# Attention and ternary feed-forward on one core: weights ahead of x rows, a second Y bank in slot 0, 32-column first-token products, M's source stored in halves, no layer norm tensor

## The reference, cut to what matters

```python
qkv = x @ w_qkv                      # 16 heads of 64; token 0 is a "first token" seen by all
# blocks of 16 tokens attend to the first token and to a causal window of their own and two
# earlier blocks (the mask leaves no later key)
attn = softmax(q k / 8)              # over the window
attn = einsum('gh,bhnij->bgnij', w_th, attn)
out  = (attn @ v) @ w_out + b_out    # row 0 of the result: v[:, 0] @ w_out + b_out
x1 = layernorm(x + out)              # eps 1e-5
h  = gelu(ternary_linear(x1, w_up))  # divides x1 by its rms + 1e-8, weights are -1, 0 or 1
y  = layernorm(x1 + ternary_linear(h, w_down))
```

## Time and profile before

| | us |
|---|---|
| median of 3 runs | 256.18 (255.93 to 256.25) |
| the profiled execution, its own time | 257.67 |
| its span, first to last instruction | 255.8 |
| PE busy in the span | 231.0 (90%) |
| DVE busy | 182.9 (72%) |
| ACT busy | 162.7 (64%) |
| POOL busy | 91.7 (36%) |
| mean granted TensorE clock | 0.978 |

### The profile page before, as it was taken

How to read it: one execution, slowest core, us unless ns; L and a number is a source line. 1 busy time by engine, 2 the same in 40 slices (tenths; PEclk the granted TensorE clock), 3 DMA queues, 4 the chain that set the end, 5 groups by cost and what they waited for, 6 DMA issues and landing times.

```text
span 255.8 us, 9953 instructions
## 1 busy us (share of the span) xinstructions
PE 231.0 (90%) x4307; PEld 206.9 (81%) x4307; DVE 182.9 (72%) x485; ACT 162.7 (64%) x311; POOL 91.7 (36%) x110
## 2 busy tenths in 40 slices
PE   7798999999999999999999899988999977899930
PEld 6697988988999898889888798877887756799920
DVE  0743689987776984688567856789568888886960
ACT  2584366687566459766887479754974444875940
POOL 7035123522322251626452543424252633012350
PEclk9999799999999999999999999999999999999995
DMA  7627560020020002010101020001001001000011
GB/s 225 194 77 222 181 162 5 3 63 3 3 55 12 23 4 67 0 24 12 54 4 41 8 65 0 23 25 40 27 0 46 3 3 42 3 12 13 3 44 41
DMA packets 18911, 11.69 MB, mean 46 GB/s; under 512 B 2036, under 2 KB 17972, under 8 KB 18740
## 3 DMA queue, kind: packets, MB, share of 16 engines
q1 hardware_dynamic: 18016, 9.94, 13.6%
q10 hardware_dynamic: 852, 1.12, 1.3%
HBM read 8.91 MB, written 2.10 MB: 43 GB/s over the span
## 4 chain that ended last, share of the span: by engine, by line
PE 50%; DVE 21%; ACT 18%; issue 4%; DMA 2%; POOL 1%; SPq 0%; POOLq 0%; DVEq 0%; ACTq 0%
PE bank L1078 8%; PE bank L1080 7%; PE bank L1079 7%; DVE CTl L851 6%; PE bank L1227 5%; PE bank L1201 5%; ACT CTh L557 3%; DVE AT L856 3%; DVE E L865 3%; ACT L648 3%; PE bank L1185 2%; DMA w_sb<-in_L_attn_w_qkv 2%; ACT Yb L557 2%; ACT E L700 2%; DVE mx L863 2%
## 5 line engine op out<-in xcount | busy, mean ns | idle before, releaser
L851 DVE TENSOR_TENSOR CTl<-bank,CTh 128x512 fp32r<-128x512 f32 x64 | 41.1, 684 | 24.2 <-ACT CTh L557 24.0
L500 POOL TENSOR_TENSOR E<-E,rc 128x400 f32<-128x400 f32 x32 | 27.9, 872 | 82.8 <-DVE rc L873 82.8
L557 ACT ACTIVATE Yb<-bank 128x512 f32<-128x512 f32 x64 | 38.5, 601 | 29.6 <-PE bank L1080 29.2
L1078 PE MATMUL bank<-xTh,Gh 128*128 128x256 f32 x128 | 40.2, 314 | 3.4 <-ACT Yb L557 2.2
L700 ACT ACTIVATE E<-E 128x400 f32<-128x400 f32 x32 | 17.3, 540 | 38.5 <-DVE E L865 38.4
L1078 PE MATMUL bank<-CTh,Mh 128*128 128x256 f32 x128 | 36.7, 287 | 1.8 <-DVE CTl L851 1.8
L1080 PE MATMUL bank<-xTh,Gl 128*128 128x256 f32 x128 | 36.2, 283 | 0.0
L1079 PE MATMUL bank<-xTl,Gh 128*128 128x256 f32 x128 | 36.1, 282 | 0.0
L557 ACT ACTIVATE CTh<-bank 128x512 fp32r<-128x512 f32 x64 | 34.7, 599 | 1.9 <-PE bank L1227 1.8
L1079 PE MATMUL bank<-CTl,Mh 128*128 128x256 f32 x128 | 35.7, 279 | 0.0
L1080 PE MATMUL bank<-CTh,Ml 128*128 128x256 f32 x128 | 35.7, 279 | 0.0
(11 more groups left out here) (142 smaller groups left out, 478.3 us busy)
## 6 DMA issues: line engine op xcount, KB each, us to landing
raw<-in_L_attn_x SPq DMA_DIRECT2D x37, 64.0 KB
pt_rows<-PT SPq DMA_DIRECT2D x1, 1024.0 KB, 6.2
R<-pt_rows SPq DMA_DIRECT2D x1, 1024.0 KB, 6.3
xr<-in_L_attn_x SPq DMA_DIRECT2D x6, 128.0 KB
out<-y SPq DMA_DIRECT2D x6, 128.0 KB, 1.8
raw<-in_L_attn_x SPq DMA_DIRECT2D x12, 56.0 KB
w_sb<-in_L_attn_w_qkv ACTq DMA_DIRECT2D x2, 256.0 KB, 4.7
w_sb<-in_L_attn_w_qkv SPq DMA_DIRECT2D x2, 256.0 KB, 5.1
```

What stands on the lines that cost most here:

```text
L500: tt(e, e, rc[s % 2][:, :].unsqueeze(2).broadcast_to([P, TILES, WIN]), ALU.mult).then_inc(s_norm, 1)
L557: copy = lambda o, i, **k: nc.scalar.activation(o, i, ACT.Copy, **k)
L851: v.tensor_tensor(ct_view(CTl[s // 4 % 2], s % 4, q), c_view(s, q), ct_view(f32(CTh[s // 4 % 2][:, :, :]), s % 4, q), ALU.subtract).then_i ...
L1078: mm(o, wh, rh, start=start, stop=False, **k)
```

## The change

Five parts. (1) On SP, w_up and w_down are loaded before the waits and transfers of `window(0, 0)`. (2) In slot 0 the second query part goes to bank 3 (`y_bank`), and the waits of `queries(0, 0)` and `queries(0, 1)` ask for one Yb copy less. (3) "v0" and "bos" use pieces of 32 columns. (4) PT is stored by two transfers of 8 heads each, the first of which waits for the first two pieces only. (5) The layer norm tensor is not formed. x1n is kept (two buffers, and two more for chunks 6 and 7), y2 = x1n * weight + down, with weight = (hroot + 1e-8) * ratio: y2 is the old one times hroot + 1e-8, and the second norm adds `floor` = 1e-5 * hden squared to the variance in place of 1e-5. `residual` makes both root inputs in one instruction and both roots are now square roots; `input_scale` has two instructions for four; `layernorm` and its calls are gone.

```diff
-            sp.wait_ge(s_eva, read_no("A", "p", 2))
-            sp.wait_ge(s_evd, read_no("D", "p", 3))
-            sp.dma_start(pt_rows.rearrange("g o c -> o g c"), PT[:, :, :]).then_inc(s_pt, 16)
-            sp.wait_ge(s_pt, 16)
+            for half in range(2):
+                sp.wait_ge(s_eva, read_no("A", "p", 2 * half))
+                sp.wait_ge(s_evd, read_no("D", "p", 2 * half + 1))
+                hs = slice(8 * half, 8 * half + 8)
+                sp.dma_start(pt_rows[hs].rearrange("g o c -> o g c"), PT[:, hs, :]).then_inc(s_pt, 16)
+            sp.wait_ge(s_pt, 32)
...
+        def y_bank(s, b):
+            return Y_BANK[b if s == 0 else 0]
...
-                    pe.wait_ge(s_Ye, 8 + 2 * s + b)
+                    pe.wait_ge(s_Ye, 8 + 2 * s + b - (s == 0))
                     c = (s // 4 + 1) % 6
-                    y_part(Y_BANK[0], slice(c * CHUNK, c * CHUNK + CHUNK), 4 * (s % 4) + 2 * b)
+                    y_part(y_bank(s, b), slice(c * CHUNK, c * CHUNK + CHUNK), 4 * (s % 4) + 2 * b)
...
-                            for lo in (0, 64):
+                            for lo in range(0, P, 32):
                                 c = P * k + lo
-                                ins = mm(bnk[lo:lo + 64, 2 * k:2 * k + 2], w_sb[2][:, c:c + 64], x0T[:, :],
+                                ins = mm(bnk[lo:lo + 32, 2 * k:2 * k + 2], w_sb[2][:, c:c + 32], x0T[:, :],
...
-                v.tensor_scalar(var_in[n % 2][:, 0, :], mv[n % 2][:, :, 1], EPS_LN, None, ALU.add).then_inc(f_vin, 1)
-                v.tensor_copy(var_in[n % 2][:, 1, :], mv[n % 2][:, :, 1]).then_inc(f_vin, 1)
+                v.tensor_tensor(var_in[n % 2][:, :, :], mv[n % 2][:, :, 1].unsqueeze(1).broadcast_to([P, 2, CT]), eps_ln[:, :, :],
+                                ALU.add).then_inc(f_vin, 1)
...
-                for i in range(CT):
-                    v.scalar_tensor_tensor(out=rms[:, i:i + 1], in0=roots[n % 2][:, 1, i:i + 1], scalar=roots[n % 2][:, 0, i:i + 1],
-                                           in1=eps_rms[:, i:i + 1], op0=ALU.mult, op1=ALU.add).then_inc(f_rms, 1)
-                dve.wait_ge(f_rms, CT * (n + 1))
-                v.reciprocal(inv[:, :], rms[:, :]).then_inc(f_inv, 1)
-                dve.wait_ge(f_inv, n + 1)
-                v.tensor_tensor(rn[:, :], inv[:, :], roots[n % 2][:, 0, :], ALU.mult).then_inc(f_rn, 1)
+                v.scalar_tensor_tensor(out=roots[n % 2][:, 1, :], in0=roots[n % 2][:, 0, :], scalar=EPS_RMS,
+                                       in1=roots[n % 2][:, 1, :], op0=ALU.mult, op1=ALU.add).then_inc(f_den, 1)
+                dve.wait_ge(f_den, n + 1)
+                v.reciprocal(scales[n % 2][:, :, :], roots[n % 2][:, :, :]).then_inc(f_scales, 1)
...
+                v.tensor_tensor(ratio[:, n % 4, :], roots[n % 2][:, 1, :], scales[n % 2][:, 0, :], ALU.mult).then_inc(f_ratio, 1)
...
+                dve.wait_ge(f_ratio, n + 1)
+                v.scalar_tensor_tensor(out=weight[:, :], in0=hroot[:, :], scalar=EPS_RMS, in1=ratio[:, n % 4, :],
+                                       op0=ALU.add, op1=ALU.mult).then_inc(f_weight, 1)
                 v.tensor_scalar(hden[:, :], hroot[:, :], EPS_RMS, None, ALU.add).then_inc(f_hden, 1)
-                dve.wait_ge(f_hden, n + 1)
-                v.reciprocal(hinv[:, :], hden[:, :]).then_inc(f_hinv, 1)
-                dve.wait_ge(f_hinv, n + 1)
-                dve.wait_ge(f_x1, CT * (n + 1))
+                dve.wait_ge(f_weight, n + 1)
...
-                    v.scalar_tensor_tensor(out=y2[own(n)][:, i:i + 1, :], in0=dn_bank(n)[:, P * i:P * i + P].unsqueeze(1),
-                                           scalar=hinv[:, i:i + 1], in1=res[own(n)][:, i:i + 1, :],
+                    v.scalar_tensor_tensor(out=y2[own(n)][:, i:i + 1, :], in0=x1n[own(n)][:, i:i + 1, :],
+                                           scalar=weight[:, i:i + 1], in1=dn_bank(n)[:, P * i:P * i + P].unsqueeze(1),
                                            op0=ALU.mult, op1=ALU.add).then_inc(f_y2, 1)
+                dve.wait_ge(f_hden, n + 1)
+                v.scalar_tensor_tensor(out=floor[:, :], in0=hden[:, :], scalar=EPS_LN, in1=hden[:, :],
+                                       op0=ALU.mult, op1=ALU.mult).then_inc(f_floor, 1)
```

More of the change, by code:

```diff
@@ L105, in attention_ffn @@
         attnS = sb("attnS", [P, CHUNK])
-        res = [sb(f"res{i}", [P, CT, P]) for i in range(2)]
-        x1n = sb("x1n", [P, CT, P])
+        res = sb("res", [P, CT, P])
+        x1n = [sb(f"x1n{i}", [P, CT, P]) for i in range(2)]
         x1Th = sb("x1Th", [P, CHUNK], F32R)
@@ L118, in attention_ffn @@
         roots = [sb(f"roots{i}", [P, 2, CT]) for i in range(2)]
-        rms, inv, rn, hss, hroot, hden, hinv, var2 = [sb(name, [P, CT]) for name in (
-            "rms", "inv", "rn", "hss", "hroot", "hden", "hinv", "var2")]
+        scales = [sb(f"scales{i}", [P, 2, CT]) for i in range(2)]
+        ratio = sb("ratio", [P, 4, CT])
+        hss, hroot, hden, weight, floor, var2 = [sb(name, [P, CT]) for name in (
+            "hss", "hroot", "hden", "weight", "floor", "var2")]
         rstd2 = [sb(f"rstd2_{i}", [P, CT]) for i in range(2)]
```

69 lines of the change are left out of this document (32 added, 37 removed).

## The result

| | before | after |
|---|---|---|
| median, 20 runs each, us | 256.34 (255.71 to 259.68) | **253.97** (252.66 to 257.69) |
| profiled execution, us | 257.67 | 253.67 |
| its span | 255.8 | 251.9 |
| mean granted clock | 0.978 | 0.979 |

The ratio is 0.9894, 95% interval 0.9869 to 0.9918: 2.4 us faster, where 2.6 was the forecast.

The account below looks back on a forecast made before the run. PE was taken to bound most slots, DVE the feed-forward steps and slots 29 and 30. Front 1.4, DVE 1.0 and end 0.2 make 2.6 us off the median 256.18: 253.6, range 252.0 to 255.3 (8 in 10).

Parts of the forecast that it names:

- the front: Start to slot 4: PE 2.65 us earlier, rows 0.7 later, slack 2.08, so a 1.27 stall and net gain 1.4.
- Second Y bank, 32 columns: PE in slots 0 and 1: the bank gains 0.85 and costs 0.35; shorter v0 and bos gain 0.65.
- The clock, 1.5: PE from 26.5 to 29.5 us: the clock stays at 2.4 GHz instead of half that, gain 1.5 us.
- The order on SP, and what waits for it: SP's loads: PT lands 0.7 us later, delaying R and chunk 1's raw rows; PE stalls 1.27 in slot 4.
- 32 columns: gain 0.65: PE's v0 and bos: 64 small pieces take 0.70 us instead of 1.02 each, gain 0.65 together.
- DVE's steps, 1.0: Feed-forward steps in slots 12, 20, 24, 28 and 30: shorter DVE work gains 1.0 us, bounds 0.5 and 1.6.
- The end, 0.2: The last two `second_sum` on DVE, behind PE's down_back: a shorter chain gains 0.2 us.
- The rows are not late: Rival, 21%: PT lands some 0.6 us sooner, PE's 2.65 arrives in full; 252.3.
- The clock falls again: Rival, 6%: low clock behind the 1.27 stall in slot 4 costs 1.5 us more; 255.1.
- DVE's savings are absorbed: Rival, 12%: shorter DVE steps only lengthen its wait for ACT's copies; 254.6.
- small pieces cost as now: Rival, 3%: v0's and bos's 64 pieces stay at 32 ns, 2.04 us each; 255.0.
- SP stands behind the 127-row piece: Rival, 8%: that issue takes 5.65 us; PT, R and raw rows come 4.6 late; 1.3 slower, 257.5.

Follow-up runs that it names:

- e04: The kernel before with only SP's order changed, w_up and w_down loaded ahead of the raw rows: 256.56 us, ratio 0.9989.
- e02: The kernel before with parts 1 to 4 (SP order, second bank, 32 columns, PT in halves), layer norm as before: 257.25 us, ratio 0.9990.
- e12: The changed kernel with products nobody reads put where PE idled in slots 29 and 30: 253.94 us, ratio 0.9892.
- e17: e07 with the two layer norm instructions put back in each of five chunks, as instructions nobody waits for: 254.77 us, ratio 0.9866.
- e14: e10 with the first token's products back on 64 columns: 252.28 us, ratio 0.9796.
- e07: The changed kernel with the first token's products (v0, bos) back on 64 columns: 252.80 us, ratio 0.9862.
- e10: The changed kernel with DVE's `ratio` and, for chunks 0 to 3, `floor` moved into its wait for the exponential: 251.91 us, ratio 0.9841.
- e03: The kernel before with the second bank in slot 0 and the 32 columns alone: 256.27 us, ratio 0.9971.
- e11: The changed kernel with slot 4's raw rows issued while SP waits for PT to land: 253.72 us, ratio 0.9903.
- e01: The kernel before with part 5 alone (DVE's, no layer norm tensor): 254.65 us, ratio 0.9915.

## Why the prediction was right, point by point

The total was right, 253.97 for 253.6, inside the range, and in good part by luck: the front alone gave nothing for 1.4, DVE's part 2.1 for 1.2, and the two errors cancel.

- **Second Y bank, 32 columns.** Right as mechanisms: no idle ahead of `queries(0, 1)`, v0 at 0.71 for 0.70, and 2.93 less from slot 0 to slot 4, for a PE that was to be 2.65 earlier. (In absolute time PE took up slot 4's transposes 1.76 earlier, at 39.70 for 41.46: 0.61 had gone ahead of slot 0 and 0.30 into the idle of slot 3.) The row of small pieces decided against the Trainium skill's overhead of each matmul (TensorEngine Tiling (Array Packing), "Performance Considerations"), by which v0 would have taken longer, not shorter; the trace gives 11 ns a piece.
- **The clock, 1.5.** It was at 1.00 in slots 0 and 1, as said, but the reason given does not hold: e04 kept the idle of 0.69 and the 1.10 of v0, and stayed at 1.00 as well. Either the low clock belongs to an execution, or the order alone removes it; one profile of each cannot tell. If the first, the sum counts it twice, once within the front's gain and its slack of 2.08, and once in the 1.49 taken off for the median. An estimate for an execution of before without it: PE takes up slot 4's transposes 1.5 earlier, the slack is 0.58, and 0.58 - 0.7 is -0.1 for the front, where e02's median gain cannot be told from zero.
- **The order on SP, and what waits for it.** Partly right. R was issued at 27.69 in e12, 28.15 in after, 29.52 in e17 and 31.26 in e02; the forecast was one number, 29.7, for what varies by over 3 us. By the prediction's own list, R before 29 was a sign of being wrong, and after's 28.15 is one. The stall stood in slot 4 in e02 (1.39), e17 (1.75), e14 (0.59) and e07 (0.31), and not in after, e10 and e12. So "net gain of the front 1.4" is the step that failed: what an execution keeps in slots 0 to 4 went from 2.93 (after) over 2.15 (e03), 0.92 (e04) and -0.57 (e02) to -0.97 (e11), and in medians the front alone gives 256.75 - 257.25, nothing, with an interval of -0.5 to +1.1 us.
- **What the step left out** is that 64 more records put other work at the boundaries of PE's instruction packets. No rival named it. In slots 2 and 3 of the kernels with 32 columns PE idled 0.30 to 2.63 for it, and it was the part of "32 columns: gain 0.65" that the term could not have.
- **DVE's steps, 1.0.** Mechanism right, size wrong. The layer norm gives nothing in the slots it stood in, as said (e17, 5.59 with and without). Five slots gave 0.29 to 0.36 each, not four with 0.27 to 0.34, and the step did not have the 0.84 of slot 24 to 25, though the row with 0.73 for hden stood in the trace of before. e01's median: 2.1 for 1.0 + 0.2.
- **The end, 0.2.** From mx of slot 31 to the end: 42.1 before, 41.8 after.
- **The rivals.** "The rows are not late" is what after's profiled execution did. "The clock falls again" at a stall in slot 4 is what e17's did. "DVE's savings are absorbed" and "small pieces cost as now" are out by e01 and by v0. "SP stands behind the 127-row piece" did not occur at that price: w_th, now directly behind that piece, stood 1.90 in issue in after (1.42 to 2.11 in the eleven kernels with the new order, 0.63 or 0.64 in the three without), and PT was issued at 22.19.

## What to carry to other kernels

A trace is one execution: where a part's gain hangs on transfers in flight, as the front's did, price it as a range over executions, and time the parts alone before believing the sum. Before an excess over the median is taken off, ask which stretch of the profile holds it, and leave that stretch out of the gain. Count the instructions an edit adds on a busy engine, not only their time: they shift the places at which the engine may run out of instructions, and it does so most where the instructions are small. A small instruction belongs where its engine waits for another anyway; two moves of that kind made the slots 1.4 us shorter.
